# A delta rule in blocks of 16 tokens on TensorE in place of a token-by-token scan on VectorE, with all sums of the first MoE awaited by attention

## The reference

```python
# layer 1: gated delta rule, 16 heads of 16 channels
q, k, v = x @ Wq + bq, x @ Wk + bk, x @ Wv + bv
k = k / (norm(k) + 1e-6);  beta = sigmoid(x @ Wbeta + bbeta)
for t in range(512):                      # a state of 16x16 for each batch and head
    delta = v[t] - S @ k[t]
    S = S + beta[t] * outer(delta, k[t])
    o[t] = S @ q[t]
x = x + o @ Wo + bo
# layer 2: MoE, top 4 of 16 experts (256 -> 2*128 -> 256), and a shared expert
# layer 3: causal attention, 16 heads of 16, q and k with rms norm and rotary embedding
# layer 4: the MoE of layer 2 once more
```

## Time and profile before

| | |
|---|---|
| median of 3 runs | 5421.66 us (5421.22 to 5442.21) |
| span of the profiled execution, first to last instruction | 5326.3 us |
| busy: TensorE, weight loads, VectorE, ScalarE, GpSimd | 3319.1, 2321.1, 3960.7, 2021.2, 1652.0 us |
| mean granted TensorE clock | 0.80 |
| chain that ended last | VectorE 45%, TensorE 30%, issue 9%, ScalarE 6%, GpSimd 5%, DMA 3% |

### The profile page before, as it was taken

How to read it: one execution, slowest core, us unless ns; L and a number is a source line. 1 busy time by engine, 2 the same in 40 slices (tenths; PEclk the granted TensorE clock), 3 DMA queues, 4 the chain that set the end, 5 groups by cost and what they waited for, 6 DMA issues and landing times.

```text
span 5326.3 us, 69075 instructions
## 1 busy us (share of the span) xinstructions
PE 3319.1 (62%) x20044; PEld 2321.1 (44%) x20044; DVE 3960.7 (74%) x9104; ACT 2021.2 (38%) x4827; POOL 1652.0 (31%) x2669
## 2 busy tenths in 40 slices
PE   6313056175561754416365888787688878887785
PEld 3101034064330643315344665565366655665574
DVE  1999988999889998999935665677566656765543
ACT  3101022132221321103123665665466656665453
POOL 1000001601516014240345214422721154326555
PEclk8655567598665986659777999999799989998998
DMA  1300000264212642136454333441223333443566
GB/s 52 130 36 7 3 12 29 81 188 128 85 35 81 183 132 84 40 108 187 124 156 134 106 100 103 139 124 45 89 88 102 100 121 116 138 124 123 185 209 201
DMA packets 409519, 562.83 MB, mean 106 GB/s; under 512 B 55616, under 2 KB 299456, under 8 KB 408512
## 3 DMA queue, kind: packets, MB, share of 16 engines
q1 hardware_dynamic: 360000, 424.14, 26.0%
q0 software_dynamic: 49152, 134.28, 7.6%
HBM read 349.80 MB, written 208.40 MB: 105 GB/s over the span
## 4 chain that ended last, share of the span: by engine, by line
DVE 45%; PE 30%; issue 9%; ACT 6%; POOL 5%; DMA 3%; SPq 0%; DVEq 0%; ACTq 0%; POOLq 0%
DVE rec L1188 5%; DVE rec L1190 5%; DVE skb L1193 5%; DVE rec L1204 4%; DVE rec L1201 4%; PE psum L1107 4%; DVE region L1196 4%; PE psum L954 3%; DVE region L1305 3%; POOL xbuck L1773 3%; PE psum L1124 2%; PE psum L898 2%; PE psum L1007 2%; PE psum L1039 2%; PE psum L976 1%
## 5 line engine op out<-in xcount | busy, mean ns | idle before, releaser
L1782 POOL DMA_INDIRECT yg<-ybuck,words x512 | 540.4, 1055 | 883.6 <-DMA ybuck<-yrow 415.4
L1107 PE MATMUL psum<-xgT,w 128*128 128x128 f32 x4400 | 633.9, 291 | 27.8 <-DMA w<-in_w13T 9.2
L1107 PEld LDWEIGHTS psum<-xgT,w 128*128 128x128 f32 x4400 | 578.0, 204 | 59.5 <-issue 48.1
L1773 POOL DMA_INDIRECT xbuck<-srow,words x512 | 527.9, 1031 | 152.5 <-issue 126.2
L886 PE MATMUL psum<-w_ident,xn 128*128 128x128 f32 x512 | 106.6, 345 | 727.0 <-ACT xn L1495 718.4
L1124 PE MATMUL psum<-w_w2T,hid 128*128 x1100 | 378.2, 427 | 285.0 <-DVE hid L1462 212.9
L1305 DVE TENSOR_REDUCE region<-psum 128x1 f32<-128x384 f32 (+3 forms) x704 | 418.4, 634 | 151.8 <-PE psum L979 149.3
L1664 ACT ACTIVATE xgT<-psum 128x256 f32<-128x256 f32 x662 | 253.3, 383 | 669.0 <-PE psum L1089 667.3
L1754 POOL TENSOR_SCALAR_AFFINE_SELECT region<-region 128x128 f32<-128x128 f32 x1024 | 286.4, 298 | 526.4 <-ACT region L1629 514.8
L1629 ACT ACTIVATE region<-psum 128x512 f32<-128x512 f32 (+3 forms) x1024 | 389.9, 453 | 156.8 <-PE psum L996 151.5
L1134 DVE SCALAR_TENSOR_TENSOR sil<-sil,psum 128x128 f32<-128x128 f32 (+1 forms) x418 | 123.5, 296 | 394.3 <-ACT sil L1679 372.3
(11 more groups left out here) (210 smaller groups left out, 7598.1 us busy)
## 6 DMA issues: line engine op xcount, KB each, us to landing
w<-in_w13T SPq DMA_DIRECT2D x550, 256.0 KB, 3.0
xg<-xbuck SPq DMA_DIRECT2D x662, 128.0 KB, 2.4
ybuck<-yrow SPq DMA_DIRECT2D x662, 128.0 KB
xbuck<-x SPq DMA_DIRECT2D x40, 512.0 KB, 5.3
x_scratch<-res SPq DMA_DIRECT2D x64, 256.0 KB, 2.1
acc<-x_scratch SPq DMA_DIRECT2D x128, 128.0 KB
xbuck<-srow,words POOLq DMA_INDIRECT x512
yg<-ybuck,words POOLq DMA_INDIRECT x512
```

Of the source, the lines that this page charges most:

```text
L1107: o = e.matmul(psum[:, mi, half], w13[I % 3][:, k, half], xgT[I % 2][:, k, :], start=(k == 0), stop=(k == 1), skip_group_check=True)
L1773: e.indirect_dma_start(xbuck[g % 2], bass.IndirectOffsetOnAxis(ap=posu[g % 2][:, J - ROWS0[g], k:k + 1], axis=0), srow[J % 2], None).then_ ...
L1782: e.indirect_dma_start(yg[y % 5], None, ybuck[g % 2][0:TILES_OF[g] * 128, :], bass.IndirectOffsetOnAxis(ap=posu[g % 2][:, j, k:k + 1], axi ...
```

## The change

The scan is replaced by a block form of the same recurrence. The host lays `x` out so that 128 rows are 16 tokens of 8 batches, so there are 64 blocks `m`: 32 stretches of 16 tokens, and for each the two groups of 8 batches in turn. With keys scaled by the root of beta, each block needs the products k.k and q.k inside the block (`d_pairs`), the inverse of a unit triangular 16x16 matrix for each batch and head (`d_row`, 15 rows by forward substitution on VectorE, for two blocks at a time), and then, in the chain that carries the state, five more steps: `s_read` (state times k and q), `s_rest`, `s_solve` (the inverse times the rest), `s_add` and `s_new` (new state), `d_out` and `s_rows` (outputs). All matmuls of them are 32x32 pieces on the diagonal of the array: weights on partitions 32x to 32x+31, output on PSUM partitions 32x to 32x+31, x from 0 to 3, all into one PSUM bank. The matrices go through DRAM to be laid out with one batch and head on each partition (`d_send`, `d_fetch`) and back (`d_back`, `d_inverse`), in runs of 16 floats.

A unit of MoE 1 is now four blocks, which is 32 tokens of all 16 batches, so every unit holds rows of every batch. `prepare(0)` now waits for `NT - 1` (63) in `added_up`, the last sum of MoE 1, where it waited for row 48. Two PSUM banks hold the states (`STATE`), so six are left to the strands where seven were. The rates change, sigmoids become tanh, and each load of a batch for attention is eight DMAs instead of one.

```diff
-HEAD_RATE, TILE_RATE, SUM_RATE, PROJECT_RATE = 0.6, 0.5, 0.35, 0.15
+HEAD_RATE, TILE_RATE, SUM_RATE, PROJECT_RATE, INVERSE_RATE = 1.4, 1.0, 0.7, 1.4, 1.1
+NT, NR, STATE = 64, 6, (6, 3)
...
+    def chain():
+        for m in range(NT):
+            while m not in prepared:
+                yield LIGHT
...
+            put("s_read", m, ai, af)
+            yield LIGHT
+            put("s_rest", m, ai)
+            yield LIGHT
...
+            put("s_solve", m, ui, uf)
+            yield LIGHT
+            put("s_took", m, ui)
...
+            if m < NT - 2:
+                put("s_add", m)
+                yield LIGHT
+                put("s_new", m)
+                yield LIGHT
+            put("d_out", m, ai)
...
+            put("s_rows", m, ai)
...
-    for q in range(NQ):
...
-        for t in range(128):
-            for part in range(3):
-                put("step", q, t, part)
-                streams[0].run(HEAD_RATE)
...
+    while not state.done:
+        state.step()
+        streams[0].run(HEAD_RATE)
+        streams[1].run(TILE_RATE)
+        streams[2].run(SUM_RATE)
+        ahead.run(PROJECT_RATE)
+        inverse.run(INVERSE_RATE)
+        zeros.run(0.5)
...
-            while 48 + b not in added_up or (b >= 6 and b + 6 not in scattered):
+            while NT - 1 not in added_up or (b >= 6 and b + 6 not in scattered):
...
+            elif name == "d_pairs":
...
+                for h in range(8 * half, 8 * half + 8):
+                    for x in range(4):
+                        p = strips(x)
+                        o = e.matmul(psum[p, mi, h % 8 * 64:h % 8 * 64 + 64], keo[p, h % 2, h // 2 * 32:h // 2 * 32 + 32],
+                                     kqT[m % NR][p, :, h // 2, :], start=True, stop=True, skip_group_check=True)
...
+            elif name == "s_solve":
...
+                for h in range(H):
+                    for x in range(4):
+                        p = strips(x)
+                        o = e.matmul(psum[p, mi, h * 16:h * 16 + 16], inv[m % NR][p, h, :], restT[p, h * 16:h * 16 + 16],
+                                     start=True, stop=True, skip_group_check=True)
...
+            elif name == "d_row":
+                n, i = u
...
+                e.tensor_tensor(tmp, bc(gram[n % 2][:, :, i, 0:i], 2, i), t[:, :, 0:i, 0:i], ALU.mult).then_inc(s["inv"], 1)
...
+                e.tensor_reduce(t[:, :, 0:i, i], tmp, AX.X, ALU.add).then_inc(s["inv"], 1)
...
+            elif name == "k_pow":
...
+                flat = f.rearrange("p a h -> p (a h)")
+                e.tensor_tensor(flat, flat, half32, ALU.pow).then_inc(s["pw"], 1)
...
+                e.tensor_tensor(vs[m % 2].rearrange("p (h e) -> p h e", e=16),
...
+            elif name == "k_split":
...
+                e.tensor_tensor(keo, bc(kqT[m % NR][:, 0, :, :].rearrange("p g t -> p (g t)"), 1, 2), bc(par2, 2, 256),
+                                ALU.mult).then_inc(s["keo"], 1)
...
+            elif name == "d_fetch":
...
+                for c in range(2):
+                    for b in range(8):
+                        src = pairs_dram[2 * n + c, 16 * b:16 * b + 16, :].rearrange("j (h t) -> h j t", h=H)
+                        e.dma_start(gram[n % 2][16 * b:16 * b + 16, c], src[:, :, b % 2 * 16:b % 2 * 16 + 16]).then_inc(
+                            s[f"fetch{n % 2}"], 16)
...
+                src = inverse_dram[m // 2].rearrange("(b h) (c a t) -> b c a h t", b=8, c=2, a=16)
+                for b in range(8):
+                    e.dma_start(inv[m % NR][16 * b:16 * b + 16, :, b % 2 * 16:b % 2 * 16 + 16], src[b, m % 2]).then_inc(
+                        s[f"inv{m % NR}"], 16)
```

648 lines of the change are left out of this document (352 added, 296 removed).

## The result

The changed kernel takes 6432.8 us (median of 4 runs, 6425.23 to 6438.84), the kernel before beside it 5425.18 us: 1.185 times as long, 95% interval 1.1828 to 1.1878. Forecast were 4970 us, and 5600 at the most. The profiled execution has a span of 6424.0 us and itself took 6425.23, so hardly more than 1 us lies around a span. The 95 us that the forecast put there are not around the program. The kernels were run in several series, each on one chip. What is compared is the ratio to the kernel before of the same series.

What follows compares the result with a forecast made beforehand. VectorE was taken to bound the scan before the change, TensorE the blocks after it. Tc of 2000 us plus 2875 us behind the blocks made a span of 4875, with 95 us around it 4970 us; range 4480 to 5600.

Steps and rivals of the forecast that it cites:

- TensorE before Tc: TensorE's work up to the last block's end: 850 us other plus 640 us new, 1490 us at full clock.
- Tc: Time from the span's start to the end of the changed program's last block, taken as 2000 us.
- The five lines: The small matmuls of `d_pairs`, `s_read`, `s_add`, `d_out` and `s_solve`: together near 640 us of TensorE.
- strips do not overlap: Rival: matmuls of different row strips cannot write one PSUM bank at a time and serialise; 6570 us, 10 in 100.
- a floor for every pair: Rival: each load and matmul pair takes 25 ns on any strip; Tc 2680 and 5650 us in all, 6 in 100.
- The clock: TensorE's mean granted clock before attention, taken as 0.88, which makes its 1490 us into 1690 us.
- low-clock rival: Small matmuls in the blocks earn less clock, mean 0.70; Tc 2600 and 5570 us in all, 8 in 100.
- TensorE was busy 82% of the stretch that it led, so Tc = 1690/0.82: First estimate of the blocks' end: the busy share from the attention half applied to TensorE's 1690 us, giving 2060 us.
- The second estimate: Blocks' end from per-block GpSimd, TensorE and VectorE times, over expert groups and the first 16 blocks: 1960 us.
- SyncE: no bound unless it waits.: Before the blocks' end: 1120 more DMAs at 0.34 us each, 380 us, or 760 at twice that, beside some 350.
- A round trip becomes the bound: Rival: the inversion's trip through DRAM, 33 us unobstructed, grows to 72 us a pair; 5270 us, 13 in 100.
- Behind the blocks: From the last block's end: 537 us to attention's first product with the values, then 2338; 2875 us.

Runs made afterwards that it cites:

- strip runs: Changed kernel with the loops over the four strips put outside in the five small products, so 16 or 32 matmuls run in a row on one strip; ratio 1.333.
- best kernel: On two queues: expert group sizes 1 and 3 swapped in order, residual's rows loaded one block ahead; ratio 0.982, again 0.977.
- the rate alone: Changed kernel with PROJECT_RATE 0.8 in place of 1.4, so the projection strand is written out at fewer stages per round; ratio 1.106.
- norm ahead: Changed kernel with load, layer norm and transposes of a pair of blocks in a strand of their own, a pair ahead; ratio 1.120.
- two blocks: On norm ahead: even and odd blocks get a projection strand each, at half the rate; ratio 1.098.
- spaced: On two blocks: `keo` moved from GpSimd to VectorE, five more empty steps behind `k_pow` and two behind `k_split`; ratio 1.045.
- late solve: On spaced: ten more empty steps ahead of `d_row`, one more between `d_pairs` and `d_keep`; ratio 1.041, in another kind of series than spaced.
- two queues: On late solve: 8 of the 16 transfers of a fetch issued from ScalarE's queue; ratio 1.030, and 1.008 in the other kind of series.
- the last step: From two queues to the best kernel: expert group sizes swapped and residual's rows loaded one block ahead; 157 us less by the medians.

## Why the prediction was wrong

- **TensorE before Tc, its price: right for the rest, too high for the new.** The five lines take 736 us in the records. The 640 of the forecast are at 2.4 GHz, 727 at its clock of 0.88; at the mean clock of 0.68 the 736 are about 500 at 2.4 GHz. The rest of TensorE's work, 1977 - 736 = 1241 us, is about 844 so (850 forecast, though 1137 us at the 0.7 named are 796). Both are estimates, since the mean clock holds for the stretch and not for these lines. The strips overlap: 128 matmuls of `s_read` in 1.93 us, where the mean clock is 0.58, are 15 ns each, and losing the alternation costs a factor of 2.8. The rivals "strips do not overlap" and "a floor for every pair" fall. They were the two for which the Trainium skill spoke. The Trainium skill, TensorEngine Tiling (Array Packing), Restrictions and Gotchas: different row tiles can't access one PSUM bank at the same time; here 128 products on four row and column strips go to one bank without being serialised. The Trainium skill, TensorE: Matmul & The Clock Gate, Part 1: never under about 25 ns from start to start; here 15, in a stretch near the lower of the clock's levels. The measurement decides.
- **The clock: wrong.** 0.68 where I took 0.88. Busy TensorE is 1977 us where 1690 were forecast; over the forecast's 82% that is 2410, 350 more than 2060. I had read the clock from the half of the old program in which TensorE is full, and argued that it would be higher than in the scan (0.69) because the busy share would be. The share was higher, 58% for 44, and the clock was not; with strip runs it stays at 0.55 even at 80% busy, as shown above. In the best kernel it is 0.78 at 71%. What decides between the two levels stays open. The low-clock rival, which laid it to small matmuls, named it with 8 in 100, and only as far as 5570.
- **"TensorE was busy 82% of the stretch that it led, so Tc = 1690/0.82": the step that failed.** The share was 58%, which makes 3415 us of 1977, 1000 us more. The 82% came from attention, where the order has much independent work. Here one generator writes a chain of dependent stages, in-order engines turn each latency into a wait for all that stands behind it, and no engine's sum tells of it. Edits that moved or spread this chain gave time: the rate alone 301 us; norm ahead 228, two blocks on it 115 more, spaced 282 more, late solve with two queues 199 more, 823 in all. Not all idle time is of this kind: 312 us of the first kind's 1447 are issue gaps (149 in the second). The second estimate, 1960 from GpSimd's and TensorE's sums, made the same mistake and so confirmed nothing.
- **GpSimd.** The power is 5.47 us (5.9 forecast), GpSimd's busy time 928 us (1160). Both sums are fine, and the bound drawn from them is not: the power costs 253 us by lying in line.
- **"SyncE: no bound unless it waits."** Its sum is no bound, but 16 more transfers a pair cost 328 us. The condition was named and not worked out.
- **"A round trip becomes the bound" (5270, 13 in 100)** was of the right kind and about the wrong loop: one that holds about 107 us a pair, through projection, power, send, fetch and norm, and not the one of the inversion, which I had at 33 us.
- **Behind the blocks: right, the closeness in part luck.** 440 us to the first projection (465), 500 to the first product (537), 2394 from there (2338), and 2894 in all (2875). In the second kind of series, the kind of the rows used, it is 432, 494, 2316 and 2810: both parts were priced a little high, and the slower series made up for it. The wait for all sums costs 205 us in the kernel before by itself (245 less 50 forecast).
- **The 95 us around the span** were a mistake by which the sum came out about 1.9% high; the span was of one kind of series and the median of the other.

What stays open: what sets the clock in the blocks; what else keeps the best kernel's TensorE at 71% in its blocks; what the late solve is worth by itself (140 us is an estimate); and how the 157 us of the last step divide between its two edits.

## What to carry to other kernels

A chain of dependent stages across in-order engines has to be added up as latency, once per turn, before any engine's busy time is: here a pair of blocks took 101 us with TensorE busy for 60, about 66 by the thread's own links and the rest by what the order put between them. If the sum of latencies exceeds the largest busy time, write the order as several turns in flight, with each consumer well behind its producer (two rounds here), transfers included, and price a wait by moving it and not by its length in the trace. A busy share or a clock read where independent work is plentiful can't be carried into such a chain.
